# Moving half of the gate and up weight blocks of the L3 feed-forward into the L3 attention, with GpSimd as helper and fewer, repeating loads

## The reference, cut to what matters

```
q = qweight[k // 8, :] >> (k % 8 * 4)[:, None] & 15        # [K, N]
z = zeros[:, n // 8] >> (n % 8 * 4)[None, :] & 15          # one row per group of 128 inputs
w = q * s[k // 128] - (z[k // 128] + 1) * s[k // 128]      # gate, up: [512, 1376]; down: [1376, 512]
y = (silu(x @ gate) * (x @ up)) @ down
```

## Time and profile before

| | us |
|---|---|
| median of 3 runs | 4417.35 |
| lowest and highest of them | 4415.72, 4435.38 |
| the profiled execution, its own time | 4429.2 |
| its span | 4427.4 |
| the attention's 16 tiles | about 3818 to 3982 |
| the feed-forward | about 3982 to 4427 |
| TensorE busy, share of the span | 86% |
| VectorE, ScalarE, POOL | 64%, 52%, 40% |

### The profile page before, as it was taken

How to read it: one execution, slowest core, us unless ns; L and a number is a source line. 1 busy time by engine, 2 the same in 40 slices (tenths; PEclk the granted TensorE clock), 3 DMA queues, 4 the chain that set the end, 5 groups by cost and what they waited for, 6 DMA issues and landing times.

```text
span 4427.4 us, 62775 instructions
## 1 busy us (share of the span) xinstructions
PE 3811.0 (86%) x21328; PEld 1913.2 (43%) x21328; DVE 2844.1 (64%) x4571; ACT 2291.2 (52%) x3974; POOL 1786.5 (40%) x1454
## 2 busy tenths in 40 slices
PE   6799995998899648999999999999999966756699
PEld 3344442333333224555555555555555533432344
DVE  6522223674576357888888898888889866566322
ACT  5422222455456436667666676766676644442222
POOL 5400000000000006778787877777787864420000
PEclk9799997889889879999999999999999988897899
DMA  3100001101100010000000000000000010005100
GB/s 108 44 1 0 0 7 35 20 1 21 20 1 1 10 56 12 19 17 7 29 1 24 12 24 13 24 13 13 23 7 23 1 60 1 26 1 137 41 10 19
DMA packets 67429, 97.53 MB, mean 22 GB/s; under 512 B 14081, under 2 KB 39689, under 8 KB 67098
## 3 DMA queue, kind: packets, MB, share of 16 engines
q1 hardware_dynamic: 67100, 93.47, 7.8%
HBM read 77.77 MB, written 6.88 MB: 19 GB/s over the span
## 4 chain that ended last, share of the span: by engine, by line
PE 63%; DVE 15%; issue 8%; ACT 6%; POOL 3%; SPq 3%; DMA 2%; DVEq 0%; POOLq 0%; ACTq 0%
PE psum L332 14%; PE psum L333 13%; PE psum L334 13%; PE psum L1282 3%; PE psum L1259 3%; DVE arena L1425 2%; PE psum L1272 2%; PE psum L2255 2%; PE psum L2243 2%; PE psum L2251 2%; PE psum L2212 2%; SPq L1205 1%; ACT xn L218 1%; PE psum L2234 1%; DVE x L1940 1%
## 5 line engine op out<-in xcount | busy, mean ns | idle before, releaser
L332 PE MATMUL psum<-xt_hi,arena 128*128 128x512 f16 (+1 forms) x2272 | 878.4, 387 | 81.3 <-DVE arena L538 24.3
L333 PE MATMUL psum<-xt_lo,arena 128*128 128x512 f16 (+1 forms) x2272 | 876.3, 386 | 0.0
L334 PE MATMUL psum<-xt_hi,arena 128*128 128x512 f16 (+1 forms) x2272 | 874.7, 385 | 0.0
L2038 POOL TENSOR_TENSOR arena<-arena 128x1024 f16<-128x1024 f16 x256 | 515.3, 2032 | 193.2 <-DVE arena L1850 148.9
L1215 POOL TENSOR_TENSOR rs<-sd,epsc 128x1 f32<-128x1 f32 x16 | 8.8, 548 | 1204.8 <-DVE sd L1469 1204.8
L1425 DVE TENSOR_REDUCE arena<-psum 128x1 f32<-128x512 f32 (+3 forms) x608 | 367.4, 654 | 188.6 <-PE psum L1262 114.7
L332 PE MATMUL psum<-arena 128*128 128x512 f16 (+1 forms) x1152 | 417.7, 367 | 82.1 <-DVE arena L2810 36.3
L1381 ACT ACTIVATE arena<-psum 128x512 f32<-128x512 f32 x576 | 324.4, 598 | 274.9 <-PE psum L1272 181.0
L333 PE MATMUL psum<-arena 128*128 128x512 f16 (+1 forms) x1152 | 417.0, 366 | 0.0
L334 PE MATMUL psum<-arena 128*128 128x512 f16 (+1 forms) x1152 | 416.7, 366 | 0.0
L332 PEld LDWEIGHTS psum<-xt_hi,arena 128*128 128x128 f16 x2272 | 225.5, 99 | 334.9 <-DVE arena L538 27.3
(11 more groups left out here) (310 smaller groups left out, 7771.7 us busy)
## 6 DMA issues: line engine op xcount, KB each, us to landing
arena<-m_wi SPq DMA_DIRECT2D x64, 320.0 KB, 2.9
arena<-arena SPq DMA_DIRECT2D x128, 64.0 KB, 2.5
arena<-m_wo SPq DMA_DIRECT2D x32, 256.0 KB, 2.6
arena<-out SPq DMA_DIRECT2D x6, 768.0 KB, 5.9
x<-L_attn_x SPq DMA_DIRECT2D x4, 1024.0 KB, 8.7
out<-x SPq DMA_DIRECT2D x4, 1024.0 KB, 4.3
arena<-gate_wT SPq DMA_DIRECT2D x16, 224.0 KB, 2.5
arena<-up_wT SPq DMA_DIRECT2D x16, 224.0 KB, 2.5
```

Source lines behind the costliest of these rows:

```text
L332: nc.tensor.matmul(out, lh, rh, start=start, stop=False)
L333: nc.tensor.matmul(out, lh, rl, start=False, stop=False)
L334: return nc.tensor.matmul(out, ll, rh, start=False, stop=stop)
L2038: nc.gpsimd.tensor_tensor(m4_ar[:, q], heads[q].broadcast_to([P, HG, P]), m4_le.unsqueeze(1).broadcast_to([P, HG, P]), ALU.mult).then_inc( ...
```

## The change

Four of the 19 pieces (gate and up, blocks 0 and 1, features 0 to 767) are made in the attention, in slots 34 to 45, twelve small steps per piece and four per slot. VectorE opens the words (`w_open`), ScalarE turns them into float16 times WS, POOL subtracts the zeros, multiplies with the scales and makes the low plane, 384 columns at a time (`w_part`), ScalarE rounds (`w_high`). The other 15 pieces stay in the feed-forward, their low planes on POOL (`pool_l3_ffn`). The words of 16 rows reach 128 partitions in one transfer whose source repeats each row 8 times: 4 transfers for a wide piece and 1 for a down piece. Zeros are kept as (z + 1) * WS in float16, which halves their bytes. For down pieces words, zeros, scales and result have two halves, and a piece's zeros and scales wait for the piece before the last. All pieces of gate and up come ahead of all of down. The buffers change sides: planes of gate and up and the loads lie where the L2 feed-forward's were.

```diff
-        A7 = 0
+        BW7 = 3 * P
+        WIDE7 = KT * BW7
+        A7 = 64080
...
+        q7 = carve(A7 + 45056, [2, WIDE7], I32)
+        q7f = carve(A7 + 57344, [WIDE7], F16)
+        w7 = carve(A7 + 60416, [WIDE7], F32)
+        z7 = carve(A7 + 66560, [WIDE7], F16)
+        s7 = carve(A7 + 69632, [WIDE7], F16)
+        hid7h = carve(0, [F3, GW], F16)
...
-        pieces7 = [(0, 0), (1, 0), (0, 1), (1, 1), (2, 0), (0, 2), (1, 2), (2, 1), (0, 3), (1, 3)]
-        pieces7 = [(m, c, 16 if m < 2 or c < F3 - 1 else (INTER - (F3 - 1) * P) // 8)
-                   for m, c in pieces7 + [(2, c) for c in range(2, F3)]]
-        BLOCK7 = [pieces7.index((1, c, 16)) + 1 for c in range(len(blocks7))]
-        BESIDE7 = [(2, 3), (4,), (5,), (6,), (7,), (8,), (9,), (10, 11), (12, 13), (14, 15), (16, 17, 18)]
+        pieces7 = [(m, c, 16) for c in range(len(blocks7)) for m in range(2)] + \
+                  [(2, c, 16 if c < F3 - 1 else (INTER - (F3 - 1) * P) // 8) for c in range(F3)]
+        EARLY7 = 4
+        BLOCK7 = [max(EARLY7, 2 * c + 2) for c in range(len(blocks7))]
+        BESIDE7 = [(4,), (5,), (6,), (7,), (8,), (9,), (10, 11), (12, 13), (14, 15), (16, 17), (18,)]
...
+            early = [(i, n) for i in range(EARLY7) for n in range(3 * KT)]
             steps = []
             add = lambda *s: steps.append(s)
+
+            def weights(n):
+                for _ in range(n):
+                    if early and t >= first + 2:
+                        i, n = early.pop(0)
+                        if n == 0:
+                            add("w_open", i)
+                        add("w_part", i, n)
+                        if n == 2 * KT - 1:
+                            add("w_high", i)
...
                    add("x_norm", z)
+                weights(2)
                 if ahead:
                     add("scores", a + 1)
...
                 if u >= 0:
                     add("add", u)
+                weights(1)
...
                 if attend:
                     add("y_out", a)
+                weights(1)
...
+                elif what == "w_part":
+                    n = f[0]
+                    cols, high, low = early7(u, n)
+                    if n < KT:
+                        if n == 0:
+                            pool.wait_ge(q7_done, u + 1)
+                            pool.wait_ge(z7_in[u % 2], 32 * (u // 2 + 1))
+                        less[n] = ch.mark(nc.gpsimd.tensor_tensor(q7f[:, cols], q7f[:, cols], z7[:, cols],
+                                                                  ALU.subtract))
+                    elif n < 2 * KT:
+                        ch.wait(less[n - KT])
+                        v = nc.gpsimd.tensor_tensor(w7[:, cols], q7f[:, cols], s7[:, cols], ALU.mult)
+                        if n == 2 * KT - 1:
+                            v.then_inc(w7_f, 1)
+                    else:
+                        pool.wait_ge(w7_h, u + 1)
+                        v = nc.gpsimd.tensor_tensor(low, w7[:, cols], high, ALU.subtract)
+                        if n == 3 * KT - 1:
+                            v.then_inc(w7_l, 1)
...
+                elif what == "w_open":
+                    act.wait_ge(w7_o, u + 1)
+                    if u:
+                        act.wait_ge(w7_f, u)
+                    nc.scalar.activation(q7f, q7[:, u % 2, :], ACT.Copy, scale=WS).then_inc(q7_done, 1)
+                elif what == "w_high":
+                    high7(act, u)
...
+                elif what == "w_open":
+                    open7(dve, ch, u).then_inc(w7_o, 1)
...
+            sp.wait_ge(s5_w, 4)
...
+                ch.link(v)
+                nc.vector.tensor_scalar(zf7[a:b, 0:8 * w], zu7[a:b, 0:w, :].rearrange("p a b -> p (a b)"), 1.0, WS, ALU.add,
+                                        ALU.mult).then_inc(z7_open, 1)
...
+        def half7(i):
+            return (i % 2) * (WIDE7 // 2) if pieces7[i][0] == 2 else 0
+
+        def after7(i):
+
+            return i - 1 if i and pieces7[i - 1][0] == 2 else i
+
+        def loads7(i):
+            return sum(KT if m < 2 else 1 for m, c, rows in pieces7[i % 2:i + 1:2])
...
-                    src = qw.rearrange("(k r) n -> r k n", r=16)[:, :, at:at + w]
-                    for j in range(8):
-                        sp.dma_start(q7[j:P:8, i % 2, 0:KT * w].rearrange("p (k n) -> p k n", k=KT), src).then_inc(q7_in[i % 2], 16)
-                    zs = zeros7_gu[m * KT:(m + 1) * KT, at:at + w]
-                    ss = sc[:, at:at + w]
-                    wide = lambda t: t[:, 0:KT * w].rearrange("p (k n) -> p k n", k=KT)
-                    spread = lambda v: v.unsqueeze(0).broadcast_to([P, KT, w])
+                    for k in range(KT):
+                        src = qw[16 * k:16 * k + 16, at:at + w].unsqueeze(1).broadcast_to([16, 8, w])
+                        sp.dma_start(q7[:, i % 2, k * w:(k + 1) * w], src).then_inc(q7_in[i % 2], 16)
+                    zs = zeros7_gu[m * KT:(m + 1) * KT, at // 2:(at + w) // 2].unsqueeze(0).broadcast_to([P, KT, w // 2])
+                    ss = sc[:, at:at + w].unsqueeze(0).broadcast_to([P, KT, w])
+                    zd = z7[:, 0:KT * w].bitcast(F32).rearrange("p (k n) -> p k n", k=KT)
+                    sd7 = s7[:, 0:KT * w].rearrange("p (k n) -> p k n", k=KT)
                 else:
-                    for j in range(8):
-                        sp.dma_start(q7[j:rows * 8:8, i % 2, 0:C], qw[16 * c:16 * c + rows, :]).then_inc(q7_in[i % 2], 16)
-                    zs = zeros7_d[c:c + 1, :]
-                    ss = sc[c:c + 1, :]
-                    wide = lambda t: t[:, 0:C]
-                    spread = lambda v: v.broadcast_to([P, C])
+                    o = half7(i)
+                    src = qw[16 * c:16 * c + rows, :].unsqueeze(1).broadcast_to([rows, 8, C])
+                    sp.dma_start(q7[0:rows * 8, i % 2, o:o + C], src).then_inc(q7_in[i % 2], 16)
+                    zs = zeros7_d[c:c + 1, :].broadcast_to([P, C // 2])
+                    ss = sc[c:c + 1, :].broadcast_to([P, C])
+                    zd = z7[:, o:o + C].bitcast(F32)
+                    sd7 = s7[:, o:o + C]
                 if i:
-                    sp.wait_ge(q7_done, i)
-                sp.dma_start(wide(z7.bitcast(F32)), spread(zs)).then_inc(z7_in, 16)
-                if i:
-                    sp.wait_ge(w7_f, i)
-                sp.dma_start(wide(s7), spread(ss)).then_inc(z7_in, 16)
+                    sp.wait_ge(w7_f, after7(i))
+                sp.dma_start(zd, zs).then_inc(z7_in[i % 2], 16)
+                sp.dma_start(sd7, ss).then_inc(z7_in[i % 2], 16)
+
+        def open7(dve, ch, i):
+            n, view, high, low = part7(i)
+            word = view(q7[:, i % 2])
+            dve.wait_ge(q7_in[i % 2], 16 * loads7(i))
+            return nc.vector.tensor_scalar(word, word, sh7[0:n, :], 15, ALU.logical_shift_right, ALU.bitwise_and)
+
+        def high7(act, i):
+            n, view, high, low = part7(i)
+            act.wait_ge(w7_f, i + 1)
+            nc.scalar.activation(high, view(w7), ACT.Copy).then_inc(w7_h, 1)
...
-                dve.wait_ge(q7_in[i % 2], 128 * (i // 2 + 1))
-                ch.link(nc.vector.tensor_scalar(word, word, sh7[0:n, :], 15, ALU.logical_shift_right, ALU.bitwise_and))
-                if i:
-                    dve.wait_ge(w7_l, 6 + i)
-                dve.wait_ge(z7_in, 32 * (i + 1))
-                nc.vector.scalar_tensor_tensor(out=w, in0=word, scalar=1.0, in1=view(z7), op0=ALU.subtract,
+                ch.link(open7(dve, ch, i))
+                dve.wait_ge(w7_l, 6 + after7(i))
+                dve.wait_ge(z7_in[i % 2], 32 * (i // 2 + 1))
+                nc.vector.scalar_tensor_tensor(out=w, in0=word, scalar=WS, in1=view(z7), op0=ALU.mult,
                                                op1=ALU.subtract).then_inc(q7_done, 1)
                 dve.wait_ge(q7_done, i + 1)
-                nc.vector.scalar_tensor_tensor(out=w, in0=w, scalar=WS, in1=view(s7), op0=ALU.mult,
+                nc.vector.scalar_tensor_tensor(out=w, in0=w, scalar=1.0, in1=view(s7), op0=ALU.mult,
                                                op1=ALU.mult).then_inc(w7_f, 1)
-                dve.wait_ge(w7_h, i + 1)
-                nc.vector.tensor_tensor(low, w, high, ALU.subtract).then_inc(w7_l, 1)
...
+        def pool_l3_ffn(pool):
+            for i in range(EARLY7, len(pieces7)):
+                n, view, high, low = part7(i)
+                pool.wait_ge(w7_h, i + 1)
+                nc.gpsimd.tensor_tensor(low, view(w7), high, ALU.subtract).then_inc(w7_l, 1)
+
         def act_l3_ffn(act):
-            def piece(i):
-                n, view, high, low = part7(i)
-                act.wait_ge(w7_f, i + 1)
-                nc.scalar.activation(high, view(w7), ACT.Copy).then_inc(w7_h, 1)
-
             def beside(f):
                 for i in BESIDE7[f]:
-                    piece(i)
-
-            for i in range(2):
-                piece(i)
+                    high7(act, i)
...
```

(28 more changed lines are left out.)

29 lines of the change are left out of this document (7 added, 22 removed).

## The result

| | us |
|---|---|
| before, median of 4 runs beside it | 4416.53 (4412.92 to 4435.38) |
| after, median of 4 runs | 4373.15 (4368.88 to 4382.13) |
| ratio | 0.9896, 95% interval 0.9864 to 0.9928 |
| profiled execution of after, its own time | 4371.3, span 4369.5 |

The kernel is 43.4 us (1.0%) faster; forecast were 44. Here is where the wait for weights went: the list of TensorE's waits after 3980 us, and its first gate and first down matmul, which answer to the earlier trace rows.

The account below looks back on a forecast made before the run. Attention was taken as bound by a chain through several engines, feed-forward by TensorE's waits for weights until the down tiles start. 61 - 16 - 1 = 44 us off 4417.4 gave 4373 us, range 4345 to 4402.

Parts of the forecast that it names:

- w_open: Attention: VectorE's shift and ScalarE's rounding delay the y norm and POOL's add; 1.7 us four times, 6.8 us lost.
- w_high: Attention: ScalarE queues behind POOL's eighth part; 2.6 us in three slots, 0.5 in slot 35, 8.3 us lost.
- Both terms: Feed-forward gain of 61 us from earlier down tiles, and attention loss of 16 us from the added steps.
- third and fourth: Feed-forward: third and fourth late pieces, 896 columns, 8.4 us each, with 5.8 for landing of zeros and scales.
- POOL beside VectorE: Feed-forward: POOL's low planes collide with VectorE's reads; 5 us taken, four meetings of 1.2 in blocks 6 to 9.
- The 45 us: Feed-forward gain if VectorE and POOL block each other entirely, by the Trainium skill's rule to the letter, instead of 61.
- Parts: Attention: ordinary POOL parts, four a slot at about 0.83 to 0.95 us each, fit its idle time and cost nothing.
- Slot 15: Attention: two more VectorE instructions on 1376 and 512 columns; 2 us at most, 1 taken.
- the rival of few engines: Repeating word transfers use few DMA engines; on one engine 330 us instead of 87, 4615 us; chance 0.05.
- POOL as the bound: Attention: POOL parts at 2.0 us make POOL the bound; loss near 59 us, 4415 us, no change; chance 0.12.
- Hidden almost wholly: Rival: waits absorb the attention's long steps (5 us) and POOL and VectorE rarely meet; 4356 us; chance 0.15.
- The signs: First gate matmul about 16 us after 3983, down tiles about 4087, 15 POOL low planes, one word transfer per down piece.

Follow-up runs that it names:

- e0: The changed kernel run again with no edit; median 4373.96 us, ratio 0.9891 to the kernel before.
- e6: e5 plus a second place for zeros and scales of the sixth and eighth piece, those of the last three wide pieces loaded a piece ahead; 4352.03 us.
- e4: The changed kernel with the low planes of the 15 late pieces back on VectorE, POOL idle in the feed-forward; 4382.04 us.
- e1: The changed kernel with two POOL parts behind the add and ScalarE's high-plane rounding moved to the end of the slot; 4373.44 us.
- e5: e1 plus VectorE's opening shift moved ahead of `o_hi` and ScalarE's opening conversion to the end of the slot before; 4363.06 us.
- e3: The changed kernel with the words in eight transfers per piece again instead of one repeating transfer; 4396.97 us.
- e9: The changed kernel with the first down piece's words held back until the eighth piece's scales have landed; 4372.51 us, one run.
- e7: The changed kernel with each of POOL's 15 late low planes made twice, first into a buffer nothing reads; 4387.40 us.

## Why the prediction was right

Both terms came out: 61 forecast and 61.1 measured, 16 forecast and 13.3 measured (13.9 in e0). In detail, from the start of TensorE's first block:

| us | forecast | measured |
|---|---|---|
| block 0 | 7.5 | 7.5 |
| first late piece ready | 5.3 | 5.2 |
| second | 10.2 | 10.0 |
| third and fourth | 16.8 | 19.8 |
| to the first down piece | 3.0 | 3.4 |
| eleven down pieces, six block changes | 37.6 | 39.6 |
| last rounding and low plane | 1.9 | 1.9 |
| POOL beside VectorE | 5 | in the rows above: 3.4 |
| sum | 87.3 | 87.5 |

- **Landings.** The sum hides two errors that cancel. I took 5.8 us for the zeros and scales of 896 columns, made from one landing of 6.48 and a smaller size. They took 6.15 and 8.12; in the other runs gate's 5.9 to 6.5 and up's 7.5 to 8.3. That is +2.7 us. The chain of before had five landings of gate's and up's scales, 6.48, 6.23, 8.64, 6.42 and 5.78 us, and I used one. Their mean, 6.7, would have given 18.6 us for the two pieces instead of 16.8; the two among them that were of 896 columns, 6.42 and 5.78, would have given 17.4, so up's 8.12 could not be read from them.
- **POOL beside VectorE.** 5 us were taken, four stretched products of 1.2. Exactly the four forecast came (blocks 6 to 9), at 0.84 each: 3.4. Line 542 was stretched four times too, by 1.85, 1.86, 0.64 and 0.65 us, but a wait for zeros and scales stood behind it each time (0.24, 0.88, 4.60 and 0.48 us were left of it), so these 5.0 us cost nothing. So the Trainium skill's rule that such instructions block each other entirely (the summary rules that the prediction names) is right for each meeting. The 45 us that it would have given were wrong because only eight of VectorE's instructions met POOL up to the last piece, and 5.0 of their 8.4 us cost nothing. The rest of the down pieces came out 2.0 - 3.4 = -1.4 against the forecast of 2.0 and 2.6 us. In e6, where most of that cover is gone, three of the four stretches of line 542 have no wait behind them and are on the path. e4 shows how little the move was worth: 1.7 to 2.7 us, with 3.4 paid for meetings.
- **`w_high`.** Forecast 2.6 in three slots and 0.5 in slot 35; measured 2.7, 3.2, 3.2 and 0.3, and 0.7 in each of two slots behind, where the granted clock was 0.67 and 0.66: 10.9 instead of 8.3. The mechanism, ScalarE queued behind POOL's eighth part, is shown by e1.
- **`w_open`.** Forecast 1.7 four times. Measured +1.2 and +2.6 in the first two, and -0.4 in each of the others, two slots behind a `w_high`: 3.1 instead of 6.8. In e1, with `w_high` away, the last two cost 0.9 each. In the first two the granted clock was 0.83 and 0.87, in e1 as well, and in e5 1.00; the prediction had a clock term for `w_high` alone. I had walked one tile and multiplied. The last two intervals, behind all steps, came out 0.6 shorter than before, which makes up the 13.3 (in the six other executions they add nothing).
- **Parts.** Forecast at nothing: held. They took 0.91 us each, and e5 places all 48, with the long steps, at a cost of 0.8 us. The 0.8 for slot 36 wasn't there (10.4 and 10.4).
- **Slot 15.** 1 us forecast, 1.3 measured: from VectorE's statistics of that slot to the next ones 8.23 us pass in after, e0 and e3, and 6.89 before. The two new instructions (line 2799) take 0.86 and 0.42.
- **Words.** One transfer reached all 128 partitions at 0.54 us of SP, and no shift waited for words in the stretch; the rival of few engines falls. POOL as the bound falls too (plain slots 7.5 to 8.7 us, forecast limit 9). "Hidden almost wholly" was wrong for the changed kernel, and e5 shows that its attention half could be had by placing two steps.
- **The signs.** The first gate matmul stood at 3985.1 and the first down matmul at 4072.6, not at 3999 and 4087, because the whole stage began earlier. Counted from the third mark they are right: 12.8 us later than 3983.1 and 47.7 earlier than 4131.1. A sign given as a time from the start of the span can't be read within the 20 us by which stages move. The others held: 15 low planes on POOL, line 2541 3 us late in three tiles, one word transfer a down piece, products of 0.69 and some of 1.53 us.
- **The median.** 4373.15 against 4373. The mechanism gives 47.7 less the 1.3 of slot 15, some 46; that the medians differ by 43.4 is within the drift, and the agreement to 0.2 us is luck.

## What to carry to other kernels

A step put into a queue costs what it and its wait exceed the idle time at its place, not its duration: 48 parts on POOL cost at most 0.8 us in all, two kinds of long steps badly placed, four times each, 12.5, so walk the queue at each place where a long step goes, not one tile. Two waits in a row hide each other's price (eight transfers instead of one cost 25.5 us in the new kernel and 7.8 in the old), so cost a part beside the others and not alone. Small operands with a single buffer set the pace of a pipeline as soon as the large ones stop doing so; give them the second buffer first (6.1 us in e6).

## What was not expected

- Zeros and scales of 896 columns, in rows of 448 bytes, landed after 6.15 us (gate) and 8.12 us (up), both later than the 1536 columns of the sixth piece, 5.84, and one of them later than 1536 columns with zeros of twice the bytes, 6.48. In e9, from 4017 to 4026 us, DMA engines were busy 20% of the time. The Trainium skill ("DMA: Bandwidth & Descriptors", Specifications, minimum transfer for line rate) wants 512 bytes or more. Whether that is the cause stays open: no run here changed the row's length alone, and in the kernel before the scales had rows of 448 bytes as well (the zeros 896) and landed in 6.42 and 5.78 us.
- Waits of TensorE of 2.5 us, once in three slots, and shorter ones at the first two `w_open` took the granted clock of the whole attention from 1.00 to 0.91 of full speed. The slot after a `w_high` ran its transposes at 1.91 instead of 1.04 us. In e1, where ScalarE's wait is 2.15 us shorter, every slot from the first `w_high` on stood at 1.00 but that of the second `w_open`, and the whole at 0.97; in e5 it stood at 1.00.
- VectorE's shift with a single tensor as input was stopped by POOL as fully as the products with two (e7).
- The start of the changed stage moves by up to 20 us between executions of nearly the same program. Distances between marks within it repeat to 1 us.
